# A last pair through banks of its own, one product per maximum, and a group quantised on GpSimd

## What is computed

```python
x = x + tanh(g_xattn[0]) * cosine(layernorm(x), ctx)        # first cross block
x = x + tanh(g_ffn[0])   * ffn_bit(layernorm(x))            # first feed-forward
x = x + tanh(g_xattn[1]) * xattn(layernorm(x), ctx, mask)   # 16 heads of 64, a null key, layer norm of the result
x = x + tanh(g_ffn[1])   * ffn_int8(layernorm(x))           # second feed-forward, inner size 352
# in ffn_int8, with one scale for the whole tensor:
scale = sigmoid(clip) * max(abs(x)) / 127
xq = clip(round(x / scale), -128, 127) * scale
h  = quant(silu(xq @ Wg.T) * (xq @ Wu.T), clip_down);  return h @ Wd.T
```

## Time and profile before

| | us |
|---|---|
| median of 3 runs | 320.3 (318.98 to 322.15) |
| the profiled execution | 321.48 |
| its span, first to last instruction | 319.6 |
| busy in the span: PE, PEld, DVE, ACT, POOL | 293.5, 238.7, 241.1, 230.0, 163.0 |
| mean granted TensorE clock | 0.984 of full |
| chain that ended last: PE, DVE, ACT, DMA | 73%, 11%, 7%, 3% |

### The profile page before, as it was taken

The page is one execution under the profiler, slowest core; times in us unless marked ns, Lnnn a source line. Parts: engine busy times, 40 slices in busy tenths (PEclk is TensorE's granted clock), DMA queues, the critical chain, the costliest instruction groups (busy, mean ns, idle before and its releaser), DMA issues.

```text
span 319.6 us, 7710 instructions
## 1 busy us (share of the span) xinstructions
PE 293.5 (92%) x2602; PEld 238.7 (75%) x2602; DVE 241.1 (75%) x722; ACT 230.0 (72%) x773; POOL 163.0 (51%) x231
## 2 busy tenths in 40 slices
PE   7788999999999869999999999999999898887595
PEld 6567768686766658998998988988989786553375
DVE  3798999999785446776877878778778776648755
ACT  2777696869899678878778878778778765239170
POOL 2124617342542135358779697885857568254000
PEclk9999999999999999999999999999999999979879
DMA  5741010002020000000000000000000000000004
GB/s 147 191 125 27 1 27 1 1 2 66 7 62 3 0 0 2 2 1 3 2 1 2 2 3 3 0 2 4 1 2 3 2 0 3 0 2 1 0 8 126
DMA packets 11478, 6.67 MB, mean 21 GB/s; under 512 B 3824, under 2 KB 10992, under 8 KB 11440
## 3 DMA queue, kind: packets, MB, share of 16 engines
q1 hardware_dynamic: 10560, 5.99, 6.8%
q10 hardware_dynamic: 880, 0.20, 0.3%
HBM read 5.14 MB, written 1.05 MB: 19 GB/s over the span
## 4 chain that ended last, share of the span: by engine, by line
PE 73%; DVE 11%; ACT 7%; issue 3%; DMA 3%; SPq 2%; POOL 1%; DVEq 0%; ACTq 0%
PE psum L1041 15%; PE psum L1168 10%; PE psum L1465 10%; PE psum L1479 9%; PE psum L1045 7%; PE psum L1047 6%; PE psum L1046 6%; PE psum L1056 3%; DVE hgm L2071 2%; DMA KT<-in_L_ffn_w_down 2%; PE psum L1558 2%; DVE nmx L1937 2%; SPq L387 2%; DVE work L1931 1%; DVE KT L2077 1%
## 5 line engine op out<-in xcount | busy, mean ns | idle before, releaser
L985 ACT ACTIVATE work<-psum,nmx 128x129 f32<-128x129 f32 x256 | 83.5, 419 | 22.8 <-DVE nmx L1937 22.8
L574 POOL TENSOR_TENSOR work<-work,rden 128x512 f32<-128x512 f32 x64 | 66.8, 1044 | 45.1 <-DVE rden L1950 44.6
L1041 PE MATMUL psum<-ident,work 128*128 128x128 f32 (+2 forms) x376 | 58.4, 281 | 2.9 <-DVE work L1931 2.6
L1937 DVE TENSOR_REDUCE nmx<-psum 128x4 f32<-128x516 f32 x64 | 41.6, 690 | 25.4 <-PE psum L1168 25.2
L985 ACT ACTIVATION_READ_ACCUMULATOR work<-psum,nmx 128x1 f32 x256 | 58.4, 228 | 0.0
L1045 PE MATMUL psum<-split 97*128 97x512 f32 (+1 forms) x128 | 52.0, 406 | 1.5 <-issue 0.8
L1041 PEld LDWEIGHTS psum<-ident,work 128*128 128x128 f32 (+2 forms) x376 | 41.3, 142 | 12.0 <-issue 3.4
L1931 DVE COPY work<-psum 128x512 f32<-128x512 f32 x64 | 43.9, 686 | 5.3 <-PE psum L1041 1.7
L1047 PE MATMUL psum<-split 97*128 97x512 f32 (+1 forms) x128 | 43.2, 338 | 0.0
L1046 PE MATMUL psum<-split 97*128 97x512 f32 (+1 forms) x128 | 43.2, 337 | 0.0
L1479 PE MATMUL psum<-work 128*128 128x128 f32 x256 | 39.0, 275 | 1.0 <-ACT work L965 1.0
(11 more groups left out here) (195 smaller groups left out, 537.0 us busy)
## 6 DMA issues: line engine op xcount, KB each, us to landing
KT<-in_L_xattn_Wkv SPq DMA_DIRECT2D x2, 384.0 KB, 4.8
X<-in_x SPq DMA_DIRECT2D x1, 768.0 KB, 5.8
out_x<-X SPq DMA_DIRECT2D x3, 256.0 KB, 2.3
work<-in_ctx SPq DMA_DIRECT2D x3, 192.0 KB, 2.5
work<-in_L_xattn_Wq SPq DMA_DIRECT2D x1, 512.0 KB, 3.5
work<-in_L_xattn_Wout SPq DMA_DIRECT2D x1, 512.0 KB, 4.0
X<-in_x SPq DMA_DIRECT2D x1, 256.0 KB, 3.3
KT<-in_L_ffn_w_gate SPq DMA_DIRECT2D x1, 256.0 KB, 5.9
```

Source lines behind the costliest of these rows:

```text
L574: pool.tensor_tensor(sx_[:, :, 0:S], sx_[:, :, 0:S], bcast(rden[n % 2][:, :], S), ALU.mult).then_inc(p_ready.sem, 1)
L985: ins = act.activation(Sx[n % 4][:, j, :], psum[:, here, (j // 2) * K1:(j // 2 + 1) * K1], ACT.Exp, bias=nmx[n % 2][:, j:j + 1], accum_out ...
L1041: return pe.transpose(dst, src, ident[0:m, 0:m])
L1937: dve.tensor_reduce(nmx[n % 2][:, :].rearrange("p (c a) -> p c a", a=2), sim, AX_X, ALU.max, negate=True).then_inc(max_done.sem, 1)
```

## The change

The last pair: the common loops stop at m = 32, and the rest is written out. The last unit (63) is normalised by VectorE, not GpSimd; its transposes go to bank 6 and are copied by ScalarE; its values go to bank 0; ScalarE copies the last values in two halves, and the projection waits for each half. The statistics read bank 7 with no copy. Centring with the gain is one instruction per batch element (VectorE, from the bank), and root and residual another. GpSimd centres pair 6 after unit 62's normalisation.

The maxima: the column of maxima, broadcast to 128 columns, times the identity puts every partition's maximum on every partition in one product, and the reduction then runs on all partitions. The filler counts become 33, 9, 26 and 12.

The last feed-forward: group 0's quantisation is in halves, all three of its hidden products are on VectorE, and GpSimd takes those of groups 1 to 3. In the last product groups 0 and 1 are quantised in halves of 256 tokens; group 2 is quantised by GpSimd (multiply-add in place, then minimum and maximum in place), and VectorE only subtracts; every group has a bank of its own, and the four outputs are scaled after the last group is quantised.

```diff
-    return f * (NC1 - 1) + c + 1
+    return c + 1 if f == 0 else NC1 + (f - 1) * (NC1 - 1) + c + 1
...
-        if in_rounds(m - 1):
-            normalise(2 * (m - 1))
-            normalise(2 * (m - 1) + 1)
+        for n in (2 * (m - 1), 2 * (m - 1) + 1):
+            if 0 <= n < NS - 1:
+                normalise(n)
         t = pair_at(m, RSTD_Y_AT)
         if t is not None:
             rstd_y(t)
-            if t < NPAIR - 1:
+            if t < NPAIR - 2:
                 y_affine(t)
         t = pair_at(m, X3_AT)
-        if t is not None and t < NPAIR - 1:
+        if t is not None:
+            if t == NPAIR - 2:
+                y_affine(t)
             y_gain(t)
             residual(t)
...
+    rstd_x(NPAIR - 2)
+    rstd_y(NPAIR - 1)
+    rstd_x(NPAIR - 1)
...
-    for f in range(NG - 1):
-        pool.wait_ge(d_copy.sem, d_copy.at(f + 1))
+    for f in range(1, NG):
+        pool.wait_ge(d_copy.sem, d_copy.at(f))
         pool.tensor_tensor(Hh[:, NC1 - 1, f * T:(f + 1) * T], up_c[f % 2], sg1[f % 2][:, NC1 - 1, :],
                            ALU.mult).then_inc(d_hp.sem, 1)
+
+
+    pool.wait_ge(gmax_v.sem, gmax_v.at(10))
+    for c in range(NC1):
+        h2 = Hh[:, c, 2 * T:3 * T]
+        pool.tensor_scalar(h2, h2, sxu[:, c:c + 1], MAGIC, ALU.mult, ALU.add).then_inc(e_p.sem, 1)
+    for c in range(NC1):
+        h2 = Hh[:, c, 2 * T:3 * T]
+        pool.wait_ge(e_p.sem, e_p.at(c + 1))
+        pool.tensor_scalar(h2, h2, MAGIC + QMAX, MAGIC - QMAX - 1.0, ALU.min,
+                           ALU.max).then_inc(e_p.sem, 1)
...
+    def last_p_evac():
+        act.wait_ge(pt_done.sem, pt_done.at(NS))
+        act.wait_ge(ot_done.sem, ot_done.at(NS - 2))
+        act.activation(PTs[(NS - 1) % 2], bank[6], ACT.Copy).then_inc(pt_last.sem, 1)
+
+    def last_o_evac(h):
+        act.wait_ge(ot_done.sem, ot_done.at(NS - 1 + h))
+        act.wait_ge(wo_done.sem, wo_done.at(NS - 2))
+        act.activation(oT[:, 2 * h * S:2 * (h + 1) * S], bank[(5, 0)[h]][:, 2 * h * S:2 * (h + 1) * S],
+                       ACT.Identity, bias=nv_col[:, 0:1]).then_inc(ot_out.sem, 1)
+
+    last_p_evac()
+    last_o_evac(0)
+    last_o_evac(1)
...
-            if f >= 2 and c < NC1 - 1:
+            if f == 2 or f > 2 and c < NC1 - 1:
                 act.wait_ge(d_h.sem, d_h.at(by_vector(f - 2, c)))
-            elif f >= 2:
-                act.wait_ge(d_hp.sem, d_hp.at(f - 1))
+            elif f > 2:
+                act.wait_ge(d_hp.sem, d_hp.at(f - 2))
             act.activation(sg1[f % 2][:, c, :], bank[1 + 2 * c], ACT.Silu,
                            scale=dq1[:, 0, c:c + 1]).then_inc(d_silu.sem, 1)
-            if c == NC1 - 1 and f < NG - 1:
+            if c == 0 and 1 <= f < NG - 1:
+                x_quantised(f + 1)
+            if c == NC1 - 1 and f > 0:
                 act.activation(up_c[f % 2], bank[2 + 2 * c], ACT.Copy).then_inc(d_copy.sem, 1)
-        if f + 2 < NG:
...
+        if g == 2:
+            continue
+        if g == 3:
+            act.wait_ge(e_cl.sem, e_cl.at(4))
+        w = T // 2 if g < 2 else T
+        for at in range(0, T, w):
+            for c in range(NC1):
+                act.activation(uh[g % 2][:, c, at:at + w], Hh[:, c, g * T + at:g * T + at + w], ACT.Identity,
+                               bias=MAGIC, scale=sxu[:, c:c + 1]).then_inc(e_u.sem, 1)
...
+        if n < NS - 1:
+            pe.wait_ge(p_ready.sem, p_ready.at(n + 1))
+            if n >= 1:
+                pe.wait_ge(pt_out.sem, pt_out.at(n))
+        else:
+            pe.wait_ge(p_last.sem, p_last.at(1))
+            pe.wait_ge(q_out.sem, q_out.at(RPP * NPAIR))
         for j in range(HPU):
-            ins = transpose(bank[4][:, j * S:(j + 1) * S], Sx[n % 4][:, j, 0:S])
+            ins = transpose(bank[4 if n < NS - 1 else 6][:, j * S:(j + 1) * S], Sx[n % 4][:, j, 0:S])
...
+        if n < NS - 1:
+            pe.wait_ge(pt_out.sem, pt_out.at(n + 1))
+        else:
+            pe.wait_ge(pt_last.sem, pt_last.at(1))
...
+            if n == NS - 1:
+                pe.wait_ge(den_done.sem, den_done.at(NS - 1))
         for j in range(HPU):
             rows = slice(DH * (j % 2), DH * (j % 2) + DH)
             at = (n % 2) * 2 * S + (j // 2) * S
-            ins = pe.matmul(bank[5][rows, at:at + S], V[:, b, HPU * hg + j, :],
+            ins = pe.matmul(bank[5 if n < NS - 1 else 0][rows, at:at + S], V[:, b, HPU * hg + j, :],
...
-        pe.wait_ge(ot_out.sem, ot_out.at(m + 1))
+        pe.wait_ge(ot_out.sem, ot_out.at(m + 1 if m < NR - 1 else NR + h))
...
+    p_transposes(NS - 2)
+    p_transposes(NS - 1)
+    for h in range(2):
+        out_proj(NR - 2, h)
+    values(NS - 2)
+    values(NS - 1)
+    for h in range(2):
+        out_proj(NR - 1, h)
...
-        transpose(bank[7][0:1, 0:P], g1[:, n:n + 1]).then_inc(gmax_t.sem, 1)
-        pe.wait_ge(gmax_v.sem, gmax_v.at(2 + 5 * n))
-        pe.matmul(bank[7][:, 0:1], ones[0:1, :], gx[0:1, n:n + 1], start=True, stop=True).then_inc(gmax_t.sem,
-                                                                                                   1)
-
-    keep_clock_long(bank[6], 36)
+        pe.matmul(bank[7][:, 0:P], g1[:, n:n + 1].to_broadcast([P, P]), ident[:, :], start=True,
+                  stop=True).then_inc(gmax_t.sem, 1)
+
+    keep_clock_long(bank[6], 33)
     global_max(0)
-    keep_clock_long(bank[6], 10)
+    keep_clock_long(bank[6], 9)
...
+            if f == 0 and b % 2 == 0:
+                pe.wait_ge(d_u.sem, d_u.at(3 + b // 2))
...
-    keep_clock_long(bank[0], 20)
+    keep_clock_long(bank[0], 26)
     global_max(1)
-    keep_clock_long(bank[0], 20)
+    keep_clock_long(bank[0], 12)
...
-            pe.wait_ge(e_out.sem, e_out.at(g - 1))
+            pe.wait_ge(e_hq.sem, e_hq.at(g + 3))
         for b in range(G):
+            if g < 2 and b % 2 == 0:
+                pe.wait_ge(e_hq.sem, e_hq.at(2 * g + b // 2 + 1))
             for c, (a, m) in enumerate(CHUNKS1):
                 for k, w in enumerate((wdT1, wd_mid, wd_low)):
-                    ins = pe.matmul(bank[g % 2][:, b * D:(b + 1) * D], hq1[g % 2][0:m, c, b * S:(b + 1) * S],
+                    ins = pe.matmul(bank[g][:, b * D:(b + 1) * D], hq1[g % 2][0:m, c, b * S:(b + 1) * S],
...
+    def last_normalise():
+
+        n = NS - 1
+        b, hg = unit(n)
+        dve.wait_ge(rden_done.sem, rden_done.at(n + 1))
+        dve.tensor_tensor(Sx[n % 4][:, :, 0:S], Sx[n % 4][:, :, 0:S], bcast(rden[n % 2][:, :], S),
+                          ALU.mult).then_inc(p_last.sem, 1)
...
+    def last_statistics():
+        dve.wait_ge(wo_done.sem, wo_done.at(NS))
+        for bb in range(2):
+            dve.bn_stats(sty[:, bb, :], last_y(bb)).then_inc(y_stats.sem, 1)
+
+    def last_centred():
+        dve.wait_ge(y_aggr.sem, y_aggr.at(2 * NPAIR))
+        dve.wait_ge(x3_done.sem, x3_done.at(NPAIR - 1))
+        for bb in range(2):
+            dve.scalar_tensor_tensor(out=yS[:, bb, :], in0=last_y(bb), scalar=mvy[:, bb, 0:1], in1=gout_bc[:, :],
+                                     op0=ALU.subtract, op1=ALU.mult).then_inc(y_centred.sem, 1)
...
-
-        t = NPAIR - 1
-        dve.wait_ge(rstdy_done.sem, rstdy_done.at(t + 1))
+        dve.wait_ge(rstdy_done.sem, rstdy_done.at(NPAIR))
         for bb in range(2):
-            ins = dve.tensor_scalar(yS[:, bb, :], yS[:, bb, :], mvy[:, bb, 0:1], rstdy[:, bb:bb + 1],
-                                    ALU.subtract, ALU.mult)
-        ins.then_inc(y_norm.sem, 1)
-        dve.wait_ge(y_norm.sem, y_norm.at(t + 1))
-        dve.tensor_tensor(yS, yS, gout_bc[:, :].rearrange("p (o d) -> p o d", o=1).to_broadcast([P, 2, D]),
-                          ALU.mult).then_inc(yg_done.sem, 1)
-        dve.wait_ge(yg_done.sem, yg_done.at(t + 1))
-        xp = X[:, 2 * t:2 * t + 2, :]
-        dve.tensor_tensor(xp, xp, yS, ALU.add).then_inc(x3_done.sem, 1)
+            dve.wait_ge(y_centred.sem, y_centred.at(bb + 1))
+            ins = dve.scalar_tensor_tensor(out=pair_row(NPAIR - 1, bb), in0=yS[:, bb, :],
+                                           scalar=rstdy[:, bb:bb + 1], in1=pair_row(NPAIR - 1, bb),
+                                           op0=ALU.mult, op1=ALU.add)
+        ins.then_inc(x3_done.sem, 1)
...
+    p_evac(NS - 2)
+    x_statistics(NPAIR - 2)
+    x_aggregate(NPAIR - 2)
+    last_statistics()
+    y_aggregate(NPAIR - 1)
+    next_norm(NPAIR - 2, 0)
+    next_norm(NPAIR - 2, 1)
+    last_centred()
+    last_output()
+    x_statistics(NPAIR - 1)
+    x_aggregate(NPAIR - 1)
+    pair_max(NPAIR - 2)
+    for bb in range(2):
+        next_norm(NPAIR - 1, bb)
+    pair_max(NPAIR - 1)
...
-        dve.wait_ge(gmax_t.sem, gmax_t.at(1 + 2 * n))
-        dve.tensor_reduce(gx[0:1, n:n + 1], bank[7][0:1, 0:P], AX_X, ALU.max).then_inc(gmax_v.sem, 1)
-        dve.wait_ge(gmax_t.sem, gmax_t.at(2 + 2 * n))
-        dve.tensor_scalar(sx[:, col:col + 1], bank[7][:, 0:1], tg[:, clip:clip + 1], 1.0 / QMAX, ALU.mult,
```

(39 more changed lines are left out.)

49 lines of the change are left out of this document (18 added, 31 removed).

## The result

The changed kernel took **318.1 us** in the median of 15 executions (314.79 to 319.89), beside 320.44 for the kernel before on the same chip (15 executions, 318.75 to 323.92). These medians differ by 2.3. The ratio of the means is 0.989 (95% interval 0.985 to 0.993), 3.5 us. The forecast was 313.4, range 311.6 to 316.8: it was too fast, and 318.1 lies outside the range. A second series gave 317.07 against 321.40, ratio 0.989 (0.985 to 0.993).

A forecast was written before the change was run, and what follows sets the result against it. The prediction took the chain of waits from about 264 us to the end as decisive, not engine shares. 5.3 ahead of S plus 1.6 gave 6.9: 314.6 against the profile, 313.4 against the 320.3 median; range 311.6 to 316.8.

The forecast's parts named there:

- S: Moment the scale of the last product is known: 302.44 before, forecast 5.3 earlier, at 297.1.
- Attention tail: Last pair's normalisation, transposes, values and projection: last projection ends 271.3 to 271.8 instead of 272.7, -1.1 (bounds -1.4 and 0).
- Copy and centring: After the last projection: L971's copy gone, -0.4; centring and gain run during GpSimd's root, -0.85.
- One product per maximum: Both global maxima: the second product (0.68) gives way to a 0.05 wait, -0.55 each, -1.1 together.
- First quantisation: From reciprocal to first SiLU, 4.4 becomes about 3.2: -1.2 at full clock, 0.2 to 0.5 with filler at half clock.
- two halves and two clamps, about 1.2: First quantisation: VectorE's time for group 0 in halves, ahead of x_transposes(0), done 1.55 after.
- Gate and up: Last feed-forward: three products at once for group 0 fill VectorE's idle time, -0.65 (bounds 0 and -0.9).
- The last product: From S to the end: halves, GpSimd's share and later outputs, -1.6 (bounds -2.35 and +2.55).
- my own absolute +15.5: Forecast end of the span counted from S, with the last output at +12.8; before it was +17.16.
- rival F: Last product: half's three rows shared unevenly, passes 0.69 and 0.42, group 2's subtraction up to 1.75; 313.9 to 314.3; chance 0.12.
- rival D: After the second maximum the clock falls, twelve fillers end at +2.4; 0 to 0.7, up to 314.1; chance 0.07.
- my 0.3: End of the last product: added because stores of groups 0 to 2 all leave within 2 us before the last output.

## Why the prediction was wrong

**Where the 4.7 us are.** The sum gave 314.6 against the profiled time, and 318.34 came. Of these 3.7 the common part holds 2.1 (the scores end at 265.58 for 263.45), the stretch to S 0.9 (34.55 for 38.99 less 5.3), the rest 0.8 (16.37 for 17.16 less 1.6). The rest is the step from the profile to the median: 1.2 in my sum, 0.24 here.

**Attention tail: right.** -1.06 for -1.1. **Copy and centring: right.** From the projection's end to the reciprocal 8.60 became 6.88; without the maximum's 0.41 that is -1.31, for -1.25.

**One product per maximum: sign right, size off.** -0.41 each for -0.55. The term that was mis-sized is the product, "some 0.1 over the transpose": it took 0.49 against 0.27. And half of the -0.41 is a draw: the 0.68 that I read in the earlier trace rows falls in a stretch at the half clock that began at 280.28, with that very product. At a full clock it is 0.47, and the saving 0.2.

**First quantisation: half.** -0.59 for -1.2 (-0.6 to -0.85 against the other profiles of before). The clock was full, as I had it. What failed is "two halves and two clamps, about 1.2". They took 1.87 (280.69 to 282.56), since I let GpSimd run beside them without a price, though the earlier trace rows showed one, and though I charged for it in the last product. With GpSimd behind, the 3.2 that I had forecast for the SiLU became 2.96.

**Gate and up: right.** 14.34 became 13.69, -0.65.

**The last product: wrong, in the sign.** -1.6 was forecast, -0.8 came against that profile, and +0.4 to +0.8 against the three others of before. Three steps failed.

The first is the baseline. I took "before" from the earlier trace rows of one execution, in which 20 filler products ran 6.05 at the half clock and held the queue to +5.05. That was itself a draw. In the other profiles TensorE starts at +3.5 to +3.9, and a full clock gives +3.19 and an end at 15.45. Then I took the whole sum off the median. The profile stood 1.2 above it; 1.2 to 1.5 of exactly this kind lay in the stage that I was replacing, so it could not be saved from the median a second time. Taken against 54.7, and with the terms to S at their 4.4, my own absolute +15.5 would have given 4.7 in all, near 315.7.

The second is the stage itself. My forecast was the fourth half at +6.6, group 3 at +9.8, TensorE's end at +11.9, the span at +15.5; measured +6.54, +10.27, +12.7, +16.37. The fourth half is right for a wrong reason: the passes took 0.69 and 0.42, not 0.56 and 0.36, but I had laid out too much waiting for GpSimd. 0.69 and 0.42 are rival F's prices, and its 1.75 for group 2 came too. The Trainium skill (Vector Engine (DVE) Microarchitecture Reference, 5.1) had the uneven share of an odd outermost count: 3 rows of 256 against 768 adjoining columns, 0.69 against 0.56, agree with it; no run tries an even number of rows. What delayed group 3 beyond that was the clock, which fell behind TensorE's 2.03 of waiting for the first half: near rival D, but in the product and not in the filler, and worth 0.6 to 0.7, its upper end. I had shortened the filler's end to +0.8 and never asked what TensorE would do until +2.8.

The third is the store: I counted the end from the last output and added 0.3. It hangs on the first. From my own group 3 at +9.8 the first store would have left at +10.5 and the span ended at +15.9 (an estimate, from the 0.69 and the 5.4 of the profile after), not +15.5. So of the 0.9 that the stage ended too late some 0.4 are the stores and 0.5 is group 3.

The exclusion of VectorE and GpSimd is shown in both places: 1.03 becomes 0.69 without GpSimd, and 1.06 becomes 0.62 with GpSimd behind. That is what the Trainium skill (SBUF — State Buffer, Who interferes with whom) states, and the trace agrees.

**Stores.** Counted from the last output, as I had done, my 0.3 was 0.4 with a low clock (2.73), and 0.7 (3.01) as soon as the last output came earlier and the first store did not.

**Left open:** why some executions draw low stretches at 12 to 24 and at 119 us. Of the twelve profiles of changed forms five have their scores end later than 264.6, of the four of before none. The clocks of before's executions reach as low (0.973), though four profiles against twelve settle nothing, so I take it for chance, but that is argued and not shown.

## What to carry to other kernels

Before a stage is replaced, take more than one profile of it: its old cost may be one execution's low clock, and what a change saves of bad luck does not come off the median. Look at the granted clock of every row that a price is read from. A rebuild that makes the first product earlier also makes TensorE wait for it; fill that wait, or the rebuild pays with the clock. Spread the last stores before shortening the work ahead of them, and count the end from the first of them where they leave together. Lay out the operands of VectorE's scaling in one run, and put GpSimd's scaling behind VectorE's, not beside it.

## What the runs showed of the hardware

- One kernel's time moves by 3 us along with the granted clock of the execution (means of 315.4 at 1.00, 318.7 at 0.978), though not with it alone (323.24 at 0.995, 321.48 at 0.979 for the kernel before), and the granted clock falls in different places in different executions.
- Group 2's subtraction, from three rows of 512 that lie far apart into one run of 1536, took 1.75 (1.74 at a full clock), and from adjoining columns 0.96. That is more than an uneven share of three rows would cost (two rows of 512 at 1.04 ns and 0.16 are 1.2); no run tells why.
- With 1 MB of output whose first three stores leave within 1.7 us, the DMA engines move some 285 GB/s without a pause and the span ends 5.4 to 5.5 after the first issue, in eight profiles of eight. With the first issued 2.3 us earlier it ends 2.36 after the last scaled output instead of 3.01.
- VectorE's wait for the f32 product with ones (one column, two passes) is 0.47 at a full clock and 0.68 at the half.
